# Self-attention loop of a decoder layer: first part ahead by one body, output product behind the scores, and who sends the third query part

## The reference, cut to what matters

```python
x = x + attn(layernorm(x), Wq, bq, Wk, bk, Wv, bv, Wo, bo)

def attn(x, ...):                        # B, S, E = 16, 256, 128; H, D = 16, 8
    q, k, v = (split_heads(x @ W + b) for W, b in ((Wq, bq), (Wk, bk), (Wv, bv)))
    scores = einsum('bhqd,bhkd->bhqk', q, k) / sqrt(D)
    # a query sees the 64 keys of its own block and 8 global tokens; the 8 global queries see all keys
    scores = where(local | is_global[:, None] | is_global[None, :], scores, -inf)
    out = einsum('bhqk,bhkd->bhqd', softmax(scores), v)
    return merge_heads(out) @ Wo + bo
```

## Time and profile before

| | us |
|---|---|
| median of 3 runs | 567.29 (566.52 to 571.22) |
| the profiled execution | 568.54 |
| its span, first to last instruction | 566.7 |
| mean granted TensorE clock | 0.961 |

### The profile page before, as it was taken

The page is one execution under the profiler, slowest core; times in us unless marked ns, Lnnn a source line. Parts: engine busy times, 40 slices in busy tenths (PEclk is TensorE's granted clock), DMA queues, the critical chain, the costliest instruction groups (busy, mean ns, idle before and its releaser), DMA issues. The chain is left out here.

```text
span 566.7 us, 17496 instructions
## 1 busy us (share of the span) xinstructions
PE 469.9 (83%) x6139; PEld 348.1 (61%) x6139; DVE 409.6 (72%) x1247; ACT 296.8 (52%) x757; POOL 298.4 (53%) x588
## 2 busy tenths in 40 slices
PE   1977888888888888888999999999767999999810
PEld 1755666666666666545676676666544888888610
DVE  7566999999888888876889898987572434434337
ACT  2573665555556656524656656564424444444237
POOL 5543454444444334201358888777771577777720
PEclk9997999999999999969999999999989999999975
DMA  6626343455655655326233333332124334333158
GB/s 189 112 51 139 55 71 63 67 132 111 110 108 110 108 107 114 81 52 150 54 83 90 95 87 97 96 85 67 34 97 132 106 110 116 110 109 98 53 178 286
DMA packets 96006, 58.30 MB, mean 103 GB/s; under 512 B 24560, under 2 KB 92224, under 8 KB 95920
## 3 DMA queue, kind: packets, MB, share of 16 engines
q1 hardware_dynamic: 74448, 39.93, 30.2%
q10 hardware_dynamic: 16896, 7.34, 6.7%
q0 software_dynamic: 4576, 9.91, 5.1%
HBM read 20.76 MB, written 17.50 MB: 68 GB/s over the span
## 5 line engine op out<-in xcount | busy, mean ns | idle before, releaser
L507 POOL TENSOR_SCALAR veps<-mv 128x2 f32<-128x2 f32 x48 | 11.2, 232 | 144.9 <-issue 101.2
L1292 ACT ACTIVATE probs<-ps 128x512 f32<-128x512 f32 x128 | 73.3, 603 | 12.1 <-PE ps L1672 9.8
L613 POOL DMA_INDIRECT expert_in<-xn,sloti x64 | 65.5, 1023 | 17.6 <-issue 17.6
L1147 DVE TENSOR_TENSOR eh<-ps,sg 128x256 f32<-128x256 f32 x40 | 17.0, 425 | 59.8 <-ACT sg L1496 58.9
L772 DVE TENSOR_REDUCE nmax<-ps 128x8 f32<-128x512 f32 x64 | 42.5, 686 | 18.9 <-PE ps L1607 18.8
L666 POOL DMA_INDIRECT expert_out<-ey,xt x40 | 38.3, 957 | 27.0 <-DVE ey L1154 16.7
L772 DVE TENSOR_REDUCE mparts<-ps 128x8 bf16<-128x512 f32 x64 | 43.3, 687 | 6.7 <-PE ps L1662 6.3
L1607 PE MATMUL ps<-kbd,qs 96*64 96x128 bf16 x512 | 38.0, 293 | 4.5 <-DMA qs<-part 3.6
L2026 PE MATMUL ps<-wgu,turned 128*128 x160 | 41.3, 380 | 0.0
L1490 ACT COPY turned<-ps 128x512 f32<-128x512 f32 (+1 forms) x43 | 23.8, 554 | 28.5 <-PE ps L2019 23.2
L509 POOL TENSOR_TENSOR rstd<-veps,minus_half 128x2 f32<-128x2 f32 x48 | 35.8, 745 | 4.0
(11 more groups left out here) (248 smaller groups left out, 1360.2 us busy)
## 6 DMA issues: line engine op xcount, KB each, us to landing
kbd<-part SPq DMA_DIRECT2D x192, 32.0 KB
qs<-part ACTq DMA_DIRECT2D x93, 64.0 KB
xt<-expert_in SPq DMA_DIRECT2D x64, 72.0 KB
qs<-part SPq DMA_DIRECT2D x51, 64.0 KB
ck_scr<-wgu SPq DMA_DIRECT2D x6, 512.0 KB
ckbd<-ck_scr SPq DMA_DIRECT2D x16, 192.0 KB
kbd<-part SPq DMA_DIRECT2D x48, 64.0 KB
wgu<-in_L_ffn_gate_up_w SPq DMA_DIRECT2D x4, 512.0 KB, 4.0
```

The lines of the kernel that those rows point to most:

```text
L613: pool.indirect_dma_start(xs, bass.IndirectOffsetOnAxis(sloti[b % 3][:, n:n + 1], 0), xn3[b % 3][:, n // TOPK, n % TOPK, :], None).then_in ...
L1292: a_.activation(probs[:, 2 * i:2 * i + 2, :], P2[i % 2][:, :].rearrange("p (j q) -> p j q", j=2), ACT.Exp, scale=SCALE).then_inc(s("probs" ...
```

## The change

`late(b)` is true for b = 0 to 13; `headed(b)` is the count of `s_("kgqg")` at which batch b's heads are masked, now that the copy of the global keys raises the same semaphore (three a batch). For these bodies:

- TensorE: the projections of batch b+2 come right behind the global keys' scores; after them the query turn, the four parts of the scores, then the output product of batch b-1, the global values, the turn of the row maxima (no longer between the last two products) and the global queries' output. The wait on `xnT` ahead of the global keys' scores is gone, since the projections wait for it.
- ScalarE: the first part of batch b+2 and its three DMA issues are in body b behind the query norm (before: at the start of body b+1, behind the key exponential).
- VectorE: the third part of batch b+1 and the last step of the global queries of batch b-1 come behind the shift copies of body b; the query maximum between the turn and the division of `attended`; `self_end` at the end of the body; the first row maximum ahead of the normalisation.
- GpSimd: the copy of the global columns behind the masking of the global keys' probabilities.
- SP: from batch 1 on it also issues the one DMA of the third query part.

```diff
+        def late(b):
+            return 0 <= b < B - 2
+        def headed(b):
+            return 3 * b + 2
...
@@ SP, regroup_self
-                        if b == 1 and Q_PART[i] == k > 0:
+                        if b > 0 and Q_PART[i] == k > (0 if b == 1 else 1):
                             sp.dma_start(qs[p][16 * i:16 * i + 16, :, :], part[:, k, 0:S]).then_inc(s_("got"), 16)
@@ GpSimd
-                last.then_inc(s_("kbg"), 1)
+                last.then_inc(s_("kgqg"), 1)
...
-                if has(b + 2):
-                    self_global_columns(b + 2)
                 if has(b):
                     pool.wait_ge(s_("gexp"), b + 1)
...
+                if has(b + 2):
+                    self_global_columns(b + 2)
@@ VectorE, attended(b, between) and self_body
                 v.transpose(turned_od, OD[:, :]).then_inc(s_("od_turned"), 1)
+                between()
                 dve.wait_ge(s_("od_turned"), b + 1)
...
                     shift_spread(b, p, lambda: global_max(b + 1) if has(b + 1) else None)
+                if late(b - 1):
+                    global_heads_out(b - 1)
+                    self_last_part(b + 1)
...
-                    attended(b - 1)
-                if b == 0:
+                    attended(b - 1, lambda: global_query_max(b) if has(b) else None)
+                elif has(b):
                     self_last_part(1)
-                if has(b):
                     global_query_max(b)
                 if has(b - 1):
                     global_rows(b - 1)
+                if has(b):
+                    global_query_sum(b)
                 if has(b + 3):
                     stats(s_, b + 3, self_arrived)
...
-                if has(b - 1):
+                if has(b - 1) and not late(b):
                     self_end(b - 1)
...
+                if late(b):
+                    self_maxima(b + 1, 0, 0)
                 if has(b + 3):
                     normalise(s_, b + 3)
...
+                if late(b):
                     self_rest(b + 2, p)
...
                     self_vg(b + 1, 1 - p)
-                    if has(b + 2):
-                        self_last_part(b + 2)
+                    if late(b):
+                        if has(b - 1):
+                            self_end(b - 1)
@@ ScalarE, self_first_part and self_body
-                at_least(act, s_("kgqg"), 2 * b - 2)
+                at_least(act, s_("kgqg"), headed(b - 2))
...
-                    self_first_part(b + 1, 1 - p)
-                    if b == 0:
-                        context_rest()
-                    queries_regrouped(b + 1, 1 - p, 0)
+                    if not late(b - 1):
+                        self_first_part(b + 1, 1 - p)
+                        if b == 0:
+                            context_rest()
+                        queries_regrouped(b + 1, 1 - p, 0)
                     self_second_part(b + 1, 1 - p)
-                    if b > 0:
-                        queries_regrouped(b + 1, 1 - p, 2)
...
                     global_query_norm(b)
+                if late(b):
+                    self_first_part(b + 2, p)
+                    queries_regrouped(b + 2, p, 0)
                 if has(b + 1):
                     self_values(b + 1, 1 - p, (1,))
@@ TensorE, self_out, global_values_out and self_body
                 pe.wait_ge(s_("att_all"), b + 1)
+                if late(b + 1):
+                    pe.wait_ge(s_("qk32"), 2 * (b + 3) + 2)
...
-                if has(b + 1):
+                if late(b):
+                    pass
+                elif has(b + 1):
                     turn_shift(s_, b + 1)
...
+                at_least(pe, s_("x_new"), b - 1)
                 if has(b + 2):
                     columns(s_, b + 2, 2)
...
                     global_keys(b, p)
-                if has(b - 1):
-                    self_out(b - 1)
-                if has(b):
+                if late(b):
+                    self_project(b + 2)
                     global_query_turn(b)
...
+                    for half in range(4):
+                        self_scores(b + 1, 1 - p, half // 2, half % 2)
+                    if has(b - 1):
+                        self_out(b - 1)
                     self_global_values(b + 1)
-                    self_scores(b + 1, 1 - p, 0, 1)
-                if has(b):
+                    turn_shift(s_, b + 1)
                     global_query_out(b, p)
-                if has(b + 1):
-                    self_scores(b + 1, 1 - p, 1, 0)
-                    self_scores(b + 1, 1 - p, 1, 1)
+                else:
...
```

## The result

The changed kernel takes 611.9 us (median of 6 runs, 610.69 to 617.05) against 567.8 (6 runs, 566.25 to 571.22): ratio 1.080, 95% interval 1.076 to 1.083. I had forecast 598 in 584 to 616. The direction and the chain on ScalarE and GpSimd came out as walked, but that chain is not what ends a body: TensorE is. So the time lies in the range, but in the part of it that the dearer rival had put there (606 to 616), above the 590 to 606 of the forecast's own case.

The account below looks back on a forecast made before the run. No engine is full; waits close the order, with ScalarE and GpSimd deciding. Thirteen cycles of 15.2 us against 12.94 add 29, body 0 and body 14 add 1 each: +31 us on 567.3, so 598, range 584 to 616.

Parts of the forecast that it names:

- the dearer rival: Slower still, 606 to 630: TensorE's clock falls in the loop, body 17.3 us at most; late landing and locked port included; 20%.
- the forecast's own case: Self loop bodies take 15.2 us against 12.94, the walk holding to within 0.6 us a body: 590 to 606; 62%.
- ScalarE's inserted first part and issues: On ScalarE, 1.82 + 1.90 us inserted ahead of the value copies: copies from 9.95, key exponential over at 11.45 us.
- signs named for "right": Bodies near 15.2 us; global scores wait for GpSimd about 1 us each; copies after issues; output product's wait gone, query turn's not.
- GpSimd's chain: Mask, columns, kbg copies and heads, 3.67 us, queue behind the key exponential; next global scores wait for them, at 15.2.
- What the change saves on TensorE: Saving on TensorE costed at nothing, hidden inside the wait for GpSimd; without that cover worth 0.69 us a body.
- closing part: TensorE's body end, global values to two last products: from 10.9 to 14.1 us, 1.1 ahead of the next global scores.
- The output product's wait: TensorE's wait for finished attention, 6.2 us in ten bodies, goes because the product now stands behind the scores.
- SP: A thirteenth DMA issue per body, 0.67 us more; landing taken as 0, at most 2.8 us; beyond that, one to one.
- VectorE: Nothing added; it stalls between its shift copies until the global scores come, and one-off early work fits its idle stretch.
- Ends: Outside the 13 cycles: body 0 adds 1 us, body 14 adds 0 to 2, taken as 1.
- The locked port: VectorE shift copies and GpSimd lock each other out, 0.4 us a body, 5 us in all; left out of the sum.

Follow-up runs that it names:

- the filled run: The changed kernel with extra TensorE products, results unused, ahead of the query turn and of the third and fourth score parts: 603.33 us, 1.063.
- the late versions: Apparently the versions with TensorE's products between the score parts again and ScalarE's first part and issues moved back (581.70 us), and further edits on it (577.05 to 581.36).
- the version with the query sum ahead: VectorE's reciprocal of the global queries' sum moved ahead of the global rows, on the version with products between score parts and ScalarE's part undone: 581.36 us, 1.022.

## Why the prediction was right in direction and short in size

**ScalarE's inserted first part and issues:** the times were right (copies at 9.90, exponential over at 11.39); what was wrong is that they decide. The issues taken back alone give 6.0 us of 44, first part and issues together 2.5, which is within the intervals. Of the signs named for "right" these held: copies only behind the issues, the output product's wait gone, the query turn's not. Two did not: bodies near 15.2 us, and a wait for GpSimd in each of them.

**GpSimd's chain:** right as a mechanism where the clock is full (14.76 with unused products). Its size was 0.45 us a body too large: the four steps took 3.2 us instead of 3.67, of which the kbg copies 0.63 where the body before the change has 1.14.

**The step that failed is TensorE's**, "What the change saves on TensorE thus lies inside the wait for GpSimd, and I cost it at nothing". I let its closing part end 1.1 us ahead of the heads. It ends 1.3 behind them (200.91 and 202.24). The term that was mis-sized is the length of the closing part, which I took at full clock: 3.2 us walked, 5.06 in the body shown, 2.97 where the clock is held. Its start I had nearly right, 10.9 walked and 11.40 on average. I had kept the clock in the dearer rival at 20%, since the earlier trace rows show a fall only after a long idle time; it fell in every body, in the one shown after three short waits. That these waits bring the fall is supported by the filled run, where less waiting went with fewer falls, but no run separates them one by one. I also saw no wait between score parts that stand in a row: it is 10.8 us in ten bodies. With ScalarE's insertion it costs little directly, since the closing part starts near the walked time all the same; without it, undoing the order that has it gave back 27.7 us, falls of the clock included. The dearer rival was the right one to add: I bounded such a body by 17.3, and it took 16.23 on average.

**The output product's wait** went, as forecast; the query turn's stayed and grew from 0.55 to 0.80 us a body. That what TensorE gains could "be worth 0.69 a body" found no support: in the order that removes the wait the score parts wait instead.

**SP** at nothing: shown by itself in the old order; in the changed kernel the scores waited for the query DMAs 0.8 us in ten bodies. **VectorE** at nothing: nothing was added, and it now stands idle 37.5 us (11 times) for the global scores. **Ends:** 1.74 for 1 in body 0, 0 for 1 in body 14. **The locked port:** left out with reason. One shift copy took 0.75 us beside GpSimd's copies and first head product, where it had taken 0.42. The kernel before, then the changed one:

```profile
143.44 0.42 DVE L783 COPY qs<-qs 32x768 bf16<-32x768 bf16 x1
```

```profile
198.80 0.63 POOL L562 COPY kbg<-kbd 96x16 bf16<-96x16 bf16 x3
198.97 0.75 DVE L792 COPY qs<-qs 32x768 bf16<-32x768 bf16 x1
```

So the Trainium skill (SBUF — State Buffer, "Who interferes with whom") agrees in kind. But in these rows VectorE paid, whose copy started second, and GpSimd's chain came out shorter than walked. The 5 us did not come.

**The split:** 24 us GpSimd's chain as it would stand at full clock, 19 the clock on TensorE's closing part with that part's later start, 1.7 body 0. It is a split by the two kernels' bodies, not a sum of causes that can be taken away one by one: taking ScalarE's part back alone returns 2.5 to 6 us, since TensorE's end lies behind it.

**Open:** why the early bodies of the late versions stay at 13.3 to 16.3 us, where VectorE's one-off work and falls of the clock come together; whether the clock can be held in all bodies, which no filling here did; and what the new places of VectorE's and GpSimd's steps cost or give, as no run put them back by themselves (two versions moved single steps of VectorE).

## What to carry to other kernels

Walk every engine's round through a loop, also the one that the edit seems to relieve, and once more with TensorE at its lower clock: the round that ends second by 1 us may be the one that decides. Putting like products in a row trades one wait for another, on whoever empties their results. Two reorderings made together should be priced as a table of four, because one may be needed only to pay for the other.

## What the runs showed of the hardware

In the changed kernel the clock fell without any long idle time. In the body shown above the waits ahead of the fall were at most 1.0 us each, and TensorE was busy 0.40 to 0.83 in each of the four us before the one in which it fell. In the kernel before, two us with 0.21 and 0.50 (173 to 175) between fuller ones left the clock at 1.00. In the version with the query sum ahead the longest wait before the fall was 1.32 us; columns as in the earlier trace rows:

```profile
185.00:186.00 1.00, 0.39 (x2) 1.00 0.33 87
186.00:187.00 1.00, 0.30 (x6) 1.00 0.80 299
...
188.00:189.00 1.00, 1.00 (x10) 0.50 0.00 0
```

The Trainium skill (TensorE: Matmul & The Clock Gate, "HAM oscillation — how this bites in real kernels") tells of a clock that falls anew in each round of a loop that waits. The changed kernel's rows agree, with a fall in every body, and I had given that rule too little weight; but the loop of that page waits for several us in each round, and here the waits were shorter. Products that nobody reads made the kernel 8.6 us faster (611.9 to 603.3). A DMA issue costs its engine time that no busy column shows: three on ScalarE hold the copies behind them for 2.0 to 2.1 us.
